# Slices of a split operand 2048 bytes apart instead of 2000, and small tensors moved, in a graph and LSTM layer

## The reference, cut to what matters

```python
# x (10000, 128), adj (10000, 10000), item_feat (10000, 128), all float32
h = item_feat @ W_item.T + b_item
b = layernorm(x) @ W_user.T + b_user
x = x + relu(adj @ h + b)                  # the adjacency stage: 400 MB of adj are read once
# an LSTM over the 10000 rows of layernorm(x), hidden size 128, zero start
hs = lstm(layernorm(x))
g = argmax(hs @ W_lin.T + b_lin, axis=-1)  # 0 or 1 for each row
w = g * hs
inc = cumsum(w)
x = x + 2.0 * hs + (inc - w) * fw_att + (inc[-1] - inc) * bw_att
```

## Time and profile before

| | |
|---|---|
| median of 3 runs | 1430.51 us (1429.76 to 1432.46) |
| profiled execution | 1429.71 us |
| its span, first to last instruction | 1427.9 us |
| mean granted TensorE clock | 0.996 |
| TensorE busy | 1402.1 us |
| VectorE busy | 1257.9 us |
| ScalarE busy | 1045.2 us |
| POOL busy | 214.0 us |
| read from memory | 432.15 MB |

### The profile page before, as it was taken

The page is one execution under the profiler, slowest core; times in us unless marked ns, Lnnn a source line. Parts: engine busy times, 40 slices in busy tenths (PEclk is TensorE's granted clock), DMA queues, the critical chain, the costliest instruction groups (busy, mean ns, idle before and its releaser), DMA issues.

```text
span 1427.9 us, 26068 instructions
## 1 busy us (share of the span) xinstructions
PE 1402.1 (98%) x7418; PEld 1205.4 (84%) x7418; DVE 1257.9 (88%) x2081; ACT 1045.2 (73%) x1429; POOL 214.0 (15%) x189
## 2 busy tenths in 40 slices
PE   8999999999999999999999999999999999999995
PEld 7888888888888888888888888888888899999995
DVE  7999999999999999999999999999999766676667
ACT  6677787787787787877877877777877676556663
POOL 0000100000001001001001001001000132026776
PEclk9999999999999999999999999999999999999998
DMA  9999999999999999999999999999999303000003
GB/s 374 364 344 375 406 389 380 399 389 381 403 380 387 402 387 387 391 389 393 393 381 401 389 377 403 390 373 404 392 384 381 131 1 144 0 2 0 0 0 145
DMA packets 143467, 442.97 MB, mean 310 GB/s; under 512 B 23945, under 2 KB 43338, under 8 KB 143308
## 3 DMA queue, kind: packets, MB, share of 16 engines
q1 hardware_dynamic: 126048, 426.43, 77.3%
q10 hardware_dynamic: 17387, 16.14, 3.7%
HBM read 432.15 MB, written 10.36 MB: 310 GB/s over the span
## 4 chain that ended last, share of the span: by engine, by line
PE 95%; DVE 3%; ACT 0%; issue 0%; DMA 0%; POOL 0%; ACTq 0%; DVEq 0%
PE psG L868 24%; PE psG L869 24%; PE psG L870 24%; PE psZ L964 10%; PE psZ L950 3%; PE psZ L952 3%; PE psZ L954 3%; DVE a_lo L1180 1%; PE psG L889 1%; PE psT L843 1%; PE psZ L970 1%; PE psI L914 1%; DVE u L1490 1%; PE psG L861 0%; DMA bi_row<-in_b_item 0%
## 5 line engine op out<-in xcount | busy, mean ns | idle before, releaser
L653 ACT ACTIVATE a_hi<-raw 128x1000 fp32r<-128x1000 f32 (+1 forms) x800 | 819.6, 1030 | 256.0 <-PE psG L870 227.4
L1180 DVE TENSOR_TENSOR a_lo<-raw,a_hi 128x1000 fp32r<-128x1000 f32 (+1 forms) x800 | 892.7, 1169 | 20.4 <-ACT a_hi L653 19.0
L868 PE MATMUL psG<-a_hi,item_hi 128*128 128x500 f32 x1560 | 617.5, 396 | 2.1 <-DVE a_lo L1180 1.2
L869 PE MATMUL psG<-a_lo,item_hi 128*128 128x500 f32 x1560 | 605.7, 388 | 0.0
L870 PE MATMUL psG<-a_hi,item_lo 128*128 128x500 f32 x1560 | 604.4, 387 | 0.0
L868 PEld LDWEIGHTS psG<-a_hi,item_hi 128*128 128x128 f32 x1560 | 293.1, 188 | 67.3 <-issue 5.4
L869 PEld LDWEIGHTS psG<-a_lo,item_hi 128*128 128x128 f32 x1560 | 293.2, 188 | 59.3 <-issue 4.4
L870 PEld LDWEIGHTS psG<-a_hi,item_lo 128*128 128x128 f32 x1560 | 292.9, 188 | 59.5
L964 PE MATMUL psZ<-hist,wh 128*128 (+1 forms) x1264 | 167.1, 275 | 2.9 <-DVE hist L1328 2.2
L964 PEld LDWEIGHTS psZ<-hist,wh 128*128 128x128 f32 x1264 | 154.0, 191 | 3.8 <-issue 2.4
L459 POOL TENSOR_TENSOR row_terms<-var,minus_half 125x4 f32<-125x4 f32 x20 | 37.6, 1879 | 662.4 <-DVE var L1136 662.4
(11 more groups left out here) (179 smaller groups left out, 845.1 us busy)
## 6 DMA issues: line engine op xcount, KB each, us to landing
raw<-in_adj_main SPq DMA_DIRECT2D x760, 500.0 KB, 6.6
raw<-in_adj_main SPq DMA_DIRECT2D x40, 250.0 KB, 5.0
sq<-rstd_copy ACTq DMA_DIRECT2D x20, 250.0 KB, 6.7
u<-x_copy SPq DMA_DIRECT2D x1, 5000.0 KB, 14.4
x_copy<-x1b SPq DMA_DIRECT2D x19, 250.0 KB, 7.1
sq<-rows_copy ACTq DMA_DIRECT2D x19, 250.0 KB, 5.7
un_bb<-rows_copy ACTq DMA_DIRECT2D x19, 250.0 KB, 7.3
u<-in_itemT SPq DMA_DIRECT2D x9, 512.0 KB, 9.9
```

Source lines behind the costliest of these rows:

```text
L653: nc.scalar.activation(a_hi[:, s % CUT, 0:n], raw[:, r % RAW, at:at + n], ACT.Copy)\
L868: pe.matmul(bank, w_hi, hi, start=(c == 0), stop=False)
L869: pe.matmul(bank, w_hi, lo, start=False, stop=False)
L1180: last = dve.tensor_tensor(a_lo[:, s % CUT, 0:m], raw[:, r % RAW, at:at + m], a_hi[:, s % CUT, 0:m].bitcast(f32), ALU.subtract)
```

## The change

The two rings become one array `a_both` of 8212 words of 4 bytes. The high ring begins at word 20 of it and the low ring at word 4116, and slices lie 512 words (2048 bytes) apart, so that 12 words between two slices stay unused. ScalarE's and VectorE's instructions remain one per half: their operands now have two runs of 500 columns. TensorE's read one run as before.

Four statistics tensors (192 bytes with their padding) are allocated between `item_hi` and `item_lo`, where `bi_row` and `item_tail` were (832 bytes). Those two become parts of `x1b`. So `item_lo` and `raw` start 640 bytes lower.

```diff
+CHUNK = 512
+HI_AT, LO_AT = 20, 4116
+SLOT_AT = tuple(s * 2 * CHUNK for s in range(4))
+PART_WORDS = 8212
...
         item_hi = sb("item_hi", [P, (CH + 1) * HID], f32r, first)
-        bi_row = sb("bi_row", [1, HID], f32, first)
-        item_tail = sb("item_tail", [P, STACKED], f32, first)
+        moments = sb("moments", [SW, SUB, 6], f32, first)
+        mean_sum = sb("mean_sum", [SW, SUB], f32, first)
+        mean_gap = sb("mean_gap", [SW, SUB], f32, first)
+        gap_sq = sb("gap_sq", [SW, SUB], f32, first)
         item_lo = sb("item_lo", [P, (CH + 1) * HID], f32r, first)
         raw = sb("raw", [P, RAW, MAXC * BW], f32, first)
-        a_hi = sb("a_hi", [P, CUT, HALF * BW], f32r, first)
-        a_lo = sb("a_lo", [P, CUT, HALF * BW], f32r, first)
+        a_both = sb("a_both", [P, PART_WORDS], f32r, first)
         xb = sb("xb", [P, 2, BW], f32, first)
         v = sb("v", [P, BW], f32, first)
         x1b = sb("x1b", [P, BW], f32, first)
+        bi_row = x1b[0:1, 0:HID]
+        item_tail = x1b[:, HID:HID + STACKED]
...
+        def chunk(at, s, i):
+
+            a = at + SLOT_AT[s % CUT] + i * CHUNK
+            return a_both[:, a:a + BW]
+
+        def chunks(at, s, n=HALF):
+
+            a = at + SLOT_AT[s % CUT]
+            return a_both[:, a:a + n * CHUNK].rearrange("p (c k) -> p c k", k=CHUNK)[:, :, 0:BW]
+
+        def by_chunk(t):
+            return t.rearrange("p (c k) -> p c k", k=BW)
...
-                nc.scalar.activation(a_hi[:, s % CUT, 0:n], raw[:, r % RAW, at:at + n], ACT.Copy)\
+                nc.scalar.activation(chunks(HI_AT, s, n // BW), by_chunk(raw[:, r % RAW, at:at + n]), ACT.Copy)\
...
-                            hi = a_hi[:, s % CUT, i * BW:(i + 1) * BW]
-                            lo = a_lo[:, s % CUT, i * BW:(i + 1) * BW]
+                            hi = chunk(HI_AT, s, i)
+                            lo = chunk(LO_AT, s, i)
...
-                last = dve.tensor_tensor(a_lo[:, s % CUT, 0:m], raw[:, r % RAW, at:at + m],
-                                         a_hi[:, s % CUT, 0:m].bitcast(f32), ALU.subtract)
+                last = dve.tensor_tensor(chunks(LO_AT, s, m // BW), by_chunk(raw[:, r % RAW, at:at + m]),
+                                         chunks(HI_AT, s, m // BW).bitcast(f32), ALU.subtract)
```

More of the change, by code:

```diff
@@ L161, in program @@
         rl = un_bb[:, 0:BW]
[L162 to L165, removed]
         spread = sb("spread", [SW, SUB], f32, first)
@@ L861, in body @@
                                 last = pe.matmul(bank, item_hi[0:STACKED, c * HID:(c + 1) * HID],
-                                                 a_hi[0:STACKED, s % CUT, i * BW:(i + 1) * BW], start=False, stop=True)
+                                                 chunk(HI_AT, s, i)[0:STACKED], start=False, stop=True)
                                 continue
-                            hi = a_hi[:, s % CUT, i * BW:(i + 1) * BW]
-                            lo = a_lo[:, s % CUT, i * BW:(i + 1) * BW]
+                            hi = chunk(HI_AT, s, i)
+                            lo = chunk(LO_AT, s, i)
                             w_hi = item_hi[:, c * HID:(c + 1) * HID]
@@ L1179, in split_lo @@
                 m = n - BW if tail else n
-                last = dve.tensor_tensor(a_lo[:, s % CUT, 0:m], raw[:, r % RAW, at:at + m],
-                                         a_hi[:, s % CUT, 0:m].bitcast(f32), ALU.subtract)
+                last = dve.tensor_tensor(chunks(LO_AT, s, m // BW), by_chunk(raw[:, r % RAW, at:at + m]),
+                                         chunks(HI_AT, s, m // BW).bitcast(f32), ALU.subtract)
                 if tail:
                     mid = slice(STACK[1], STACK[1] + TAIL)
-                    last = dve.tensor_tensor(a_hi[mid, s % CUT, m:n], raw[mid, r % RAW, at + m:at + n],
-                                             a_hi[mid, s % CUT, m:n].bitcast(f32), ALU.subtract)
+                    short = chunk(HI_AT, s, 1)[mid]
+                    last = dve.tensor_tensor(short, raw[mid, r % RAW, at + m:at + n], short.bitcast(f32),
+                                             ALU.subtract)
                 last.then_inc(lo_ready, 1)
```

## The result

The changed kernel takes 1434.19 us (median of 20 runs, 1432.69 to 1436.68), the kernel before beside it 1430.66 us (20 runs, 1429.44 to 1433.56). The ratio is 1.0021, with a 95% interval of 1.0015 to 1.0027: slower by 3.5 us, where 17.8 us less were forecast. The profiled execution took 1434.49 us, span 1432.7, granted clock 0.995.

What follows compares the result with a forecast made beforehand. TensorE's 4680 adjacency matmuls were taken as the bound. 1429.7 less 17.8 us (3.8 ns each), all else 0, gave 1411.9; with 0.8 for the median 1412.7, say 1413 us; range 1400 to 1437.

Steps and rivals of the forecast that it cites:

- What bounds: Adjacency stage lasts as long as TensorE's 4680 matmuls of 500 columns, started one after the other, 225.4 ns apart.
- Places: Adjacency matmuls: price goes with a slice's place in the ring; the change gives all eight slice 1's two remainders.
- what slice 1 does not fix: Low ring to high item part (144, then 16), high to low of one slice; gain 4.0 cut to 3.8 ns.
- Worth: Gain per adjacency matmul: from 225.7 to 221.7 ns, taken as 3.8 ns, 17.8 us over 4680.
- second case: Slice 1 behind a slice whose last matmul took 382: durations 383, 386, 382, or 221.7 ns each.
- Split in two runs, DMA, small tensors: ScalarE's and VectorE's splits 0 to 10 ns longer, hidden by waits; DMA cost 0; small tensors 0 us.
- A: Rival: adjacency slices settle on a bad rhythm, if three durations exceed 1163; +2 ns, +9 us, 1440; 17%.
- B: Rival: adjacency price comes from other engines' and DMA's memory access; no change, 1428 to 1433 us; 12%.
- C: Rival: all adjacency matmuls at 382, -27 us, and VectorE comes to bind; 1405 us; 15%.
- second term: C's cost: VectorE holds TensorE 84 ns in each of 18 blocks, 1.5 us.
- The 0.19 us lead: VectorE's lead over TensorE behind a block's statistics; from 4.0 ns saved per matmul VectorE binds.
- D: Rival: slice 1 in its slow variant, 388, 386, 382; gain 2.4 ns, 11 us, 1419 to 1420; 14%.

Runs made afterwards that it cites:

- e3: Changed kernel with all three of slice 1's distances (16, 144, 208) given to every slice; 1432.21 us beside 1432.73 for the kernel before.
- e14: Kernel before with the small tensors moved and the shared memory alone, slices still 2000 bytes apart; 1433.53 us beside 1431.85.
- e5: The probe: changed kernel with 1096 matmuls added at the end, other engines idle; 1675.87 us beside 1429.97 for the kernel before.
- e2: Changed kernel with raw alone 64 bytes higher, rings kept in place; 1434.54 us beside 1432.73 for the kernel before.
- e10: Changed kernel with all three products at distance 192 by the remainder of 256; 1421.27 us beside 1429.74 for the kernel before.
- e15: e10 with v and two layer norm steps for 16 of 500 columns after the first block; adjacency period 53.55 us, whole time 67422 us not to be read.
- e9: Changed kernel with all three products at distance 144 by the remainder of 256; 1433.39 us beside 1429.74 for the kernel before.

## Why the prediction was wrong

*What bounds.* Right. The stage is the sum of its matmul steps; the loss equals 4680 steps at 0.75 ns.

*Places.* The remainders were right, and so was the forecast that all eight slices would be alike once they were the same for all. But the price does not go with the place alone: before, slice 1 took 221.3 to 227.0 ns from pass to pass. One of the two remainders that were named as slice 1's was, however, of a product that is never computed: low part with low item part. Of the three products run, the change kept one of slice 1's distances (16) and changed two (144 to 16, 208 to 80 by 256). The text had put these under "what slice 1 does not fix" and taken 0.2 ns for them.

*Worth.* Here it failed: "After the change each slice follows one with slice 1's remainders, so the second case should repeat." The second case was one of two sets of durations of the same three matmuls, and that they differed with what came ahead of them was itself the sign that a slice has no price of its own. e3 gives every slice all three distances of slice 1 and takes 226.00 ns instead of 221.7. The forecast of -3.8 ns meant 221.9; 226.54 was measured, 4.6 ns or 21 us more. Three parts make it up. 1.2 ns: the case taken was the rarer one; the L868 of 382 or 383 before 386 and 382 comes in 37 of slice 1's 170 passes, and its mean is 223.1. 2.9 ns: slice 1's distances without the other slices between them (e3). 0.5 ns: the two distances that the change did not keep, put at 0.2. The second is the main one.

*Split in two runs, DMA, small tensors.* 1195 and 1041 ns, unchanged; 389 GB/s against 390; VectorE's lead at the tight place of a block is some 0.2 us as before. All zero, as said. In e14 the moved tensors cost 0.11 us a block, and its step, 0.53 ns longer on 234 matmuls, accounts for that: they cost through the distances they shift, not through themselves.

*The rivals.* A happened: no averaging, and one product that pays 393. It is not the one that A suspected: the low part with the high item slice (L885) became the cheapest, 385, and the low item slice with the high part (L886) pays. A's size was +2 ns, taken from a made-up trio of 388, 393, 388; the change's own sum of 387, 385 and 393 is 1165, just over the 1163 from which A was said to decide. The measured 1434.19 us lies between 1400 and 1437 only because that range reached into A; the forecast of 1408 to 1416 and its direction were wrong. A could have had more than 17%: 13 of the probe's 16 distances cost 223 to 229 ns and the mean over all 16 is 225.4, close to the old kernel's 225.8, and a single place is more often above that than below. That the old kernel simply averages over places is a reading of this, not shown, since the sequence counts as well. B is refuted by e5, and e2 agrees: no other engine takes part. C exists, at another place, and its second term was far too small. 84 ns in each of 18 blocks was the price; e10 has a period of 54.24 where 5.05 ns x 234 matmuls under 54.78 would be 53.60, 0.64 us per block, 12 us in all, and e15's 53.55 confirms that as VectorE's. The 0.19 us lead had been counted at one place. In e10 TensorE starts 54 or 55 ns behind the end of VectorE's split, the least such distance in the trace, at three halves (0, 16 and 38) of every one of blocks 2 to 18; in the kernel before the medians there were 286, 183 and 514 ns. D would have been e3; it does not hold either, though D's 223.3 ns was close to what slice 1 took on the mean, 223.1.

The text set against itself the Trainium skill, SBUF — State Buffer, Who interferes with whom: "PE and ACT never wait on anyone". For the other engines that agrees with e5, where idle neighbours leave 388, 385, 393 as they were. But TensorE's two operands do cost each other time by their distance, 220.0 to about 229 ns for the same instruction. The Trainium skill, TensorE: Matmul & The Clock Gate, Back-to-back issue gap, gives N/2.4 + 2.5 as the gap of an isolated matmul, 210.8 ns for 500 columns; the prediction set it against a steady stream of them. Undisturbed steps of this stage and the probe average 220.0 ns at the least.

## What to carry to other kernels

A price read at one place of a sequence holds only with its neighbours, and one pass may be its rarer case, so take the mean of all passes; before giving it to all, run that sequence by itself behind the kernel, with the same walk over both operands. Making all places alike ends a mixture, so it can settle above it as well as below: try arrangements in which consecutive matmuls keep one distance, and several of them: of the four distances tried here that way, two were cheap. When a step that binds gets shorter, list every place where the next engine's lead is short, not only the shortest.

## What the hardware showed unexpectedly

- A matmul of 500 float32r columns, repeated on the same two operands, costs 220.0 to about 229 ns from start to start, by the distance of the two modulo 256 bytes, with everything else idle at a granted clock of 0.99.
- At distance 0, one of the dear ones, 512 columns cost 226.6 ns, no more than 500; 384 cost 173.3, 256 cost 120.0, 128 cost 111.8.
- Equal instructions at equal distances come in different durations (382 to 393) in e9, in e3 and in the probe, where one pair of operands alone runs 222, 231, 233 ns in turn, so the sequence has a state. What this state is stays open; so does why 144 is cheap with one item slice and dear on a walk over them.
